# First layer of a two-layer adapter kernel in steps of two groups of batches instead of one

## What is computed

```python
W = weights[condition]                       # 64 x 64 per batch, 16 of them to choose from
c = einsum('bct,bcd->bdt', x, W)             # mixes the 64 tokens of a batch
logits = c @ router_w.T + router_b           # 8 experts
probs = softmax(logits); topv, topi = top_k(probs, 2)
gates = topv / sum(topv)
w = zeros(N, 8) with w[n, topi[n]] = gates[n]
h = einsum('nd,erd->ner', c, A)              # 8 experts x rank 16
out = einsum('ner,eor->no', h * w[:, :, None], Bm) * 0.5
x = x + out
```

## Time and profile before

| | us |
|---|---|
| median of 3 runs (1154.43 to 1160.8) | 1154.85 |
| the profiled execution's own time | 1155.02 |
| its span, first to last instruction | 1153.4 |
| PE busy | 1095.3 (95%) |
| DVE busy | 684.0 (59%) |
| ACT busy | 502.4 (44%) |
| POOL busy | 221.9 (19%) |
| mean granted TensorE clock | 0.989 of full speed |
| last add of the first layer (store issued) | 157.9 from the start |

### The profile page before, as it was taken

One profiled execution on the slowest core, in us unless ns is written; L12 is line 12 of the kernel. 1 busy time (PEld: TensorE's weight loads), 2 busy tenths in 40 slices (PEclk: granted clock), 3 DMA queues, 4 the chain that ended last, 5 costly groups with the idle time before them and its releaser, 6 DMA issues.

```text
span 1153.4 us, 21547 instructions
## 1 busy us (share of the span) xinstructions
PE 1095.3 (95%) x5801; PEld 916.0 (79%) x5802; DVE 684.0 (59%) x1321; ACT 502.4 (44%) x1027; POOL 221.9 (19%) x354
## 2 busy tenths in 40 slices
PE   4899979999999899999999999999999999999998
PEld 4899967888878688778888778777777788888886
DVE  4788953472745628463555486835555466656666
ACT  1112213563745637463565472135555444444443
POOL 2111110020201102010111000055554232222210
PEclk9899989999999999999999999999999999999999
DMA  6489855393665828475664442269999899999995
GB/s 214 165 299 336 274 213 184 113 355 122 237 246 178 286 79 303 157 260 211 220 227 152 152 121 74 73 206 352 356 350 346 334 394 354 334 365 328 314 332 201
DMA packets 114924, 283.09 MB, mean 245 GB/s; under 512 B 17202, under 2 KB 22322, under 8 KB 112946
## 3 DMA queue, kind: packets, MB, share of 16 engines
q1 hardware_dynamic: 85232, 178.95, 44.1%
q0 software_dynamic: 29216, 102.91, 25.6%
q10 hardware_dynamic: 418, 0.53, 0.2%
HBM read 181.65 MB, written 100.70 MB: 245 GB/s over the span
## 4 chain that ended last, share of the span: by engine, by line
PE 65%; DVE 12%; DMA 9%; issue 5%; ACT 3%; SPq 3%; DVEq 1%; ACTq 1%; POOL 0%; POOLq 0%
PE psum L1451 15%; PE psum L1453 15%; PE psum L1452 15%; PE psum L1545 4%; PE psum L1650 3%; PE psum L1651 3%; DMA xp<-act_scratch 3%; DMA out<-x1t 2%; PE psum L1537 2%; DVE x1g L1057 2%; PE psum L1546 2%; PE psum L1461 1%; ACT w L833 1%; PE psum L1659 1%; SPq L503 1%
## 5 line engine op out<-in xcount | busy, mean ns | idle before, releaser
L1451 PE MATMUL psum<-base_hi,xp_hi 128*128 128x512 f32 x512 | 204.7, 400 | 4.8 <-DVE xp_lo L1189 2.7
L1453 PE MATMUL psum<-base_hi,xp_lo 128*128 128x512 f32 x512 | 200.2, 391 | 0.0
L1452 PE MATMUL psum<-base_lo,xp_hi 128*128 128x512 f32 x512 | 200.2, 391 | 0.0
L1451 PE MATMUL psum<-w,xp_hi 128*128 128x512 f32 x448 | 183.5, 410 | 3.1 <-DVE xp_lo L1107 2.4
L1453 PE MATMUL psum<-w,xp_lo 128*128 128x512 f32 x448 | 178.2, 398 | 0.0
L1452 PE MATMUL psum<-w,xp_hi 128*128 128x512 f32 x448 | 177.9, 397 | 0.0
L647 POOL DMA_DIRECT2D raw<-w1T x112 | 59.1, 528 | 437.7 <-DVE w L1089 414.1
L1089 DVE TENSOR_TENSOR w<-raw,w 128x1024 fp32r<-128x1024 f32 x112 | 132.4, 1221 | 14.3 <-ACT w L768 8.0
L815 ACT ACTIVATE xp_hi<-xp 128x256 fp32r<-128x256 f32 x124 | 51.4, 417 | 180.4 <-PE psum L1453 171.3
L1189 DVE TENSOR_TENSOR xp_lo<-xp,xp_hi 128x256 fp32r<-128x256 f32 x124 | 52.0, 425 | 119.9 <-ACT xp_hi L815 119.7
L1451 PEld LDWEIGHTS psum<-base_hi,xp_hi 128*128 128x128 f32 x512 | 96.3, 188 | 30.3 <-issue 5.8
(11 more groups left out here) (278 smaller groups left out, 1952.3 us busy)
## 6 DMA issues: line engine op xcount, KB each, us to landing
raw<-w1T POOLq DMA_DIRECT2D x120, 512.0 KB, 6.5
delta_scratch<-dl SPq DMA_DIRECT2D x80, 512.0 KB, 4.3
xp<-act_scratch SPq DMA_DIRECT2D x74, 256.0 KB, 3.2
act_scratch<-yT SPq DMA_DIRECT2D x72, 256.0 KB, 2.5
act_scratch<-x1g SPq DMA_DIRECT2D x16, 1024.0 KB, 5.2
x1t<-act_scratch SPq DMA_DIRECT2D x64, 256.0 KB, 4.8
out<-x1t SPq DMA_DIRECT2D x62, 256.0 KB, 5.0
xg<-xT SPq DMA_DIRECT2D x15, 1024.0 KB, 8.1
```

The lines of the kernel that those rows point to most:

```text
L1451: mm(out, a_hi, b_hi, start=start, stop=False, skip_group_check=True)
L1452: mm(out, a_hi, b_lo, start=False, stop=False, skip_group_check=True)
L1453: return mm(out, a_lo, b_hi, start=False, stop=stop, skip_group_check=True)
```

## The change

The first layer goes in NS = 8 steps of two groups. The gates of two groups are one chain of small operations on 128 x 32 elements (18 with the two bias additions) and four `hw0`. The mixing result has two banks (1 and 7), the transposed hidden values two halves of bank 2. In step n PE turns groups 2n and 2n+1, projects 2n+3, mixes 2n+2, expands 2n with the mixing of 2n+3 behind its first quarter, expands 2n+1 and projects 2n+4. The loops over steps are written out.

Beside it: the ring of x has six buffers (XRING); `index_3` and the reading of its sums (`index_read`) stand ahead of the first gates; `w0tab` is loaded by SyncE behind x of group 0, and no longer by ScalarE after the first half of it has landed; ScalarE makes the exponent of the next gates ahead of its later projection copy; POOL's early load for the second layer waits for the adds of groups 0 to 11, as its buffer is shared with the ring.

```diff
-RING = 4
+XRING = 6
+NS = NG // 2
+GS = 2 * GT
...
-            act.wait_ge(xg_first[0], 16)
-            for h in range(2):
-                act.dma_start(w0tab[h * C:(h + 1) * C, :], w0).then_inc(w0_in, 16)
...
+            for n in range(NS):
+                h0_high(n)
...
+                if n < NS - 1:
+                    z_copy(2 * n + 3)
+                    if NS - 5 <= n:
+                        w_high(2 * (n - NS + 5), 16)
+                        w_high(2 * (n - NS + 5) + 1, 16)
+                    gates_exp(n + 1)
+                if n < NS - 2:
+                    z_copy(2 * n + 4)
...
-            def step0(g, slot):
-                gates0(g + 1)
-                add_x(g, slot, 0)
-                hidden_low(g + 1)
-                add_x(g, slot, 1)
...
+            for n in range(NS - 1):
+                hidden_low(2 * n)
+                hidden_low(2 * n + 1)
+                if n == 0:
                     index_4()
+                else:
+                    add_x(2 * n - 1, 1)
+                if n == NS - 2:
+                    gates0(n + 1)
+                add_x(2 * n, 0)
+                add_x(2 * n, 1)
+                if n == 1:
+                    dve.wait_ge(const_split_hi, 2)
+                    second_layer_constants()
+                if n < NS - 2:
+                    gates0(n + 1)
+                    add_x(2 * n + 1, 0)
+                if NS - 5 <= n < NS - 2:
+                    w_low(0, 2 * (n - NS + 5))
+                    w_low(0, 2 * (n - NS + 5) + 1)
...
+            def two_groups(n):
+                if n < NS - 1:
+                    turn_h0(n)
+                    z_of(2 * n + 3, 0)
+                    y_of(2 * n + 2)
+                    z_of(2 * n + 3, 1)
+                    if n == 0:
+                        pe.wait_ge(const_split, 1)
+                expand(2 * n)
+                if n == NS - 2:
+                    turn_h0(n + 1)
+                expand(2 * n + 1)
+                if n < NS - 2:
+                    z_of(2 * n + 4, 0)
+                    z_of(2 * n + 4, 1)
```

More of the change, by code:

```diff
@@ L409, in _ @@
                 sp.dma_start(xg[0][:, ks, :], xT[0, :, ks, :]).then_inc(xg_first[q], 16)
+            for h in range(2):
+                sp.dma_start(w0tab[h * C:(h + 1) * C, :], w0).then_inc(w0_in, 16)
             load_x(1, 1)
             sp.dma_start(b0raw[:, :], b0T).then_inc(b0_in, 16)
-            for g in range(2, RING):
+            for g in range(2, 4):
                 load_x(g, g)
@@ L615, in w0_blocks @@
                     w0_block(2 * t + s, s)
-            for g in range(RING):
+            for g in range(4):
                 if g >= 2:
@@ L700, in _ @@
             act.activation(b0_hi[:, :], b0raw[:, :], ACT.Copy).then_inc(const_split_hi, 1)
[L701 to L709, removed]
+            z_copy(1)
+            gates_exp(0)
+            z_copy(2)
+            for n in range(NS):
+                h0_high(n)
+                if n == 0:
+                    act.wait_ge(const_in, 16 * 2)
+                    act.activation(q2[:, :, 0:Z1], q1raw[:, :, :], ACT.Copy).then_inc(const_split_hi, 1)
+                if n < NS - 1:
[6 more added lines that the diff above has]
+                    z_copy(2 * n + 4)
             def x_high(j, half):
@@ L1071, in _ @@
             index_2()
+            index_3()
+            index_read()
             dve.wait_ge(rbias_in, 16)
@@ L1483, in y_of, with expand @@
                 last.then_inc(yz_done, 1)
-            def group0(g, slot, last_group=False):
-                if not last_group:
-                    z_of(g + 1, (slot + 1) % RING, 0)
-                pe.wait_ge(hw0_ready, 2 * g + 2)
-                if not (isinstance(g, int) and g == 0):
-                    pe.wait_ge(h0_lo_done, g)
-                for m in range(GT):
-                    last = pe.transpose(h0T_ps[:, m * P:(m + 1) * P], hw0[:, m, :], ident[:, :])
-                last.then_inc(h0T_done, 1)
-                if not last_group:
-                    z_of(g + 1, (slot + 1) % RING, 1)
-                if isinstance(g, int) and g == 0:
-                    pe.wait_ge(const_split, 1)
+            def expand(g):
@@ new lines, in turn_h0 @@
+            def turn_h0(n):
+                pe.wait_ge(hw0_ready, GS * (n + 1))
+                if n > 0:
+                    pe.wait_ge(h0_lo_done, 2 * n)
+                for m in range(GS):
+                    last = pe.transpose(h0T_of(2 * n + m // GT)[:, m % GT * P:(m % GT + 1) * P], hw0[:, m, :],
+                                        ident[:, :])
+                last.then_inc(h0T_done, 1)
+            def two_groups(n):
[4 more added lines that the diff above has]
+                    z_of(2 * n + 3, 1)
+                    if n == 0:
+                        pe.wait_ge(const_split, 1)
[6 more added lines that the diff above has]
+                    z_of(2 * n + 4, 1)
```

223 lines of the change are left out of this document (120 added, 103 removed).

## The result

The changed kernel takes 1143.8 us in the median of 4 runs (1142.0 to 1146.36), the kernel before 1157.82 beside it (4 runs, 1154.43 to 1161.34): a ratio of 0.988, 95% interval 0.9835 to 0.9925. It is faster by a little over 1%, 13 to 14 us where 15.6 were forecast, and 1143.8 lies within the range. One launch of the kernel before, beside e1 to e4, took 1810.3 us at a mean granted clock of 0.557 and enters no ratio. The profiled execution took 1142.0 us with a span of 1140.4; the one before 1155.02 and 1153.4, so like against like gives 13.0 us.

A forecast was written before the change was run, and what follows sets the result against it. VectorE was taken to set the pace in late groups, and a loop of PE and VectorE early. A last add 16.8 us earlier, less 1.2 of allowances, gained 15.6: 1155.0 to 1139.4 us, range 1136.5 to 1145.5.

The forecast's parts named there:

- Bound: Middle of the first layer: the two-group step becomes PE's own work, with gates hidden by 1.0 us to spare.
- PE's step: PE's work on two groups: transposes 0.5, half projections 7.08, mixings 0.84, expansions 6.06; 14.48 us in all.
- Gates: VectorE's paired chain: small operations at 0.223 us make 3.98, four `hw0` 0.80; 4.8 us for two groups.
- Start: Before the first step: the 4.14 us wait for the mixing matrices goes, first transposes at 29.6.
- Constants: Step 1: the second layer's constants, 2.23 us, stand ahead of the gates; PE waits 1.3 us.
- End: From step 6: PE waits 2.9 us, then VectorE sets the pace; last add at 141.1, 16.8 us earlier.
- Allowances: Clock after the new 2.9 us wait, 0 to 2 us, and DMAs, 0 to 3.6; 1.2 taken for both.
- The sum: Whole launch: a gain of 15.6 us from 1155.0 gives 1139.4 us.
- B: Rival: DMAs bound the early steps, 15.7 us a step, 3.6 us over three steps; 1141.8 us; chance 0.13.
- rival E: Rival: x of odd groups lands late, PE waits in five steps from 11 us landing; 1173 us at 14.7; chance 0.04.
- C: Rival: gates longer than thought, setting the step from 5.8 us on; 6.5 us less gain, 1145.9 us; chance 0.07.
- D: Rival: the start gives less, PE's idle time there could be 4 us more; 1143.5 us; chance 0.06.

The follow-up runs named there:

- e1: Changed kernel with a result-neutral reduction repeated four times in every chain of gates, some 0.9 us more each; 1151.03 us in one run.
- e4: Changed kernel with ScalarE's exponent of the next gates behind its later projection copy; 1157.04 us in one run.
- e2: Changed kernel with fourteen repeats of a reduction in every chain of gates, some 3.1 us more each; 1171.62 us, 1.0112 times the kernel before.
- e5: Changed kernel with `w0tab` loaded by ScalarE's queue again, behind the wait for x's first half; 1148.01 us in one run.
- f1: Kernel before with only the load of `w0tab` moved to SyncE's queue behind x's first tile; 1153.66 us, 0.996 times the kernel before.
- e7: Changed kernel with the second layer's vector constants behind the adds of their step instead of ahead; 1146.75 us in a single run.
- f3: Changed kernel with the second layer's vector constants behind their step's adds, timed in six runs; 1143.37 us, 0.9866 times the kernel before.
- e3: Changed kernel with four buffers of x instead of six; 1275.62 us in one run.
- f2: Changed kernel again without an edit; 1145.85 us in six runs, 0.9888 times the kernel before.
- e8: Changed kernel with VectorE's last two `w_low` behind the last adds; no launch time given, last add 0.1 us earlier against the first transposes.
- e6: Changed kernel with a step's second mixing ahead of the even group's first expansion quarter; 1152.86 us.

## Why the prediction was right, and where its sizes were off

T, S and L are those of the prediction: the end of a step's second mixing, the start of its transposes, and the last add.

*Bound.* Right: PE's step sets the pace of the middle and the gates are hidden in it. e1 shows that 0.9 us more gates cost the middle nothing, e2 that 3.1 cost 2.0. No DMA bounds it.

*PE's step* was the mis-sized term: 14.48 forecast, 14.95 measured. The transposes of four came to 0.74, outside the bounds of 0.28 to 0.56; the four half projections to 7.41, not 7.08, since the half behind the transposes takes 1.93 and the full one 3.71; mixings 0.88 for 0.84; the expansions 5.92, less than 6.06. The rows of single groups, added up, don't give the step; 0.33 us of the difference shows only in steps that begin without a wait. What sets it isn't shown.

*Gates.* Right: 4.04 + 0.80 = 4.84 for the 4.8 forecast, a small operation 0.22 to 0.23 us for 0.223, near the lower bound of 0.207. The value was a choice between two bounds far apart (0.207 and 0.32), so that it came to the third digit is luck. They start at T + 3.05 (2.95) and PE returns at T + 8.83 (8.80).

*Start.* 29.69 for 29.6, but by luck in part: other executions of the same code have 29.97 to 31.39. The order of the steps was right (mixing 0 at 19.22, index sums from 20.10, gates from 24.59). What the table's new place is worth was wrong: in the paired start e5 shows 0.3 us for it, and f1 shows that its 4.5 could be had without any pairing.

*Constants.* 1.3 forecast, 1.22 measured, and e7 shows that they are the cause.

*End.* Step 6's T came at 126.20, not 123.5, by the steps' length and T being 6.12 behind S, not 5.68. From there the last add took 18.0, not 17.6: 0.26 of the difference is a wait for a store. The PE wait was 2.82 for 2.9. So L = 144.2 for 141.1, and the forecast's own sign, a last store at 141 to 143, was missed.

*Allowances.* 1.2 us for the clock and the DMAs. In the first profile the clock stayed up and 0 was due, and that was luck. From the last transposes to the end of the last add it took 12.79 us there; in the other executions with the same order and the same wait, at a clock of 0.50 to 0.83 in the stages behind it, it took 13.17 (e5), 13.39 (f3), 13.40 (e3, e4, e7) and 14.26 (f2). So the clock costs 0.4 to 1.5 us here, within the 0 to 2 of the forecast. The rule of the Trainium skill, page "TensorE: Matmul & The Clock Gate", part "The HAM clock gate", pointed the right way in these six and wasn't borne out by the first profile.

*The sum.* By profiles, 3.1 later at L, less 1.2 not used, and 0.7 lost in the second layer: 2.6 us, the difference between 1139.4 and 1142.0. The medians differ by more (1143.8), since the level it started from was low: the median of the kernel before, 1154.85 in three runs, is 1157.82 in four and 1158.69 in seventeen. The gain, which doesn't depend on the level, was 14.0 and 12.8 by the medians, for 15.6.

*Rivals.* B: the DMA share was 1.01 from 80 to 88 us, yet PE waits for no tile of x. Landing grew, and the loads, issued ahead into a ring of six, covered it. The issues from 84 to 108 us, answering to the earlier trace rows:

```profile
act_scratch<-x1g SPq DMA_DIRECT2D x3, 1024.0 KB, 7.2
xg<-xT SPq DMA_DIRECT2D x3, 1024.0 KB, 9.2
raw<-w1T POOLq DMA_DIRECT2D x2, 512.0 KB, 6.5
```

A load lands in 9.2 us, 8.1 before, and rival E needed 11 to begin. C would have needed gates longer by 1 us. C's price, 1145.9, lies above the range's end of 1145.5, which was said to take it in. The lower end doesn't come out of its own terms either: without the allowance and with a chain shorter by 0.25 us in the three places where it shows, the sum is about 1137.4, not 1136.5. D's price of 4 us at the start didn't come; a variation of 1.7 us did, from the first projection. E became real only in e3, when the ring was four. The earlier place of `index_3` and POOL's later load weren't tried by themselves.

*A rule on the DMAs.* The stage from 12 to 24 us of the changed kernel, in which nearly only loads run:

```profile
12.00:24.00 12.00, 11.25 (x93) 10.31 (x93) 6.66 (x36) 1.85 (x3) 2.79 (x12) 1.00 1.01 403
```

So this core alone moves 403 GB/s from DRAM for 12 us, and 361 with loads and stores mixed from 44 to 52. The Trainium skill, page "DMA: Bandwidth & Descriptors", section "Where 436 GB/s comes from", lets the DRAM side bind near 358 GB/s, while its section "Measured" has 425 for a core alone. By the rows the first is no ceiling for one core; the 403 is nearer to the second.

## What to carry to other kernels

Where an engine's long chain of small dependent operations sits in a loop with another engine, make the chain once for two units of work: eighteen operations on twice the elements cost 4.04 us where two chains cost 7.04, and the pairing pays as long as the chain ends before the other engine returns. Check what the pairing doubles elsewhere (buffers: the ring of four cost 130 us) and where a short operation stands behind a copy that waits for the end of the step (13.5 us). Take the cheap part by itself first: 0.4% of the time, a third of this gain, was to be had by the place of one transfer.

## What the runs showed of the hardware

*The first projection runs at half rate for a time that differs between executions.* Its 32 matmul records took 5.41 us in the first profile, 6.97 in e7. Two stages of 1 us of f2:

```profile
12.00:13.00 1.00, 1.00 (x6) 1.00 (x6) 0.83 (x6) 0.00 (x0) 0.00 (x0) 1.00 0.98 369
...
15.00:16.00 1.00, 1.00 (x11) 1.00 (x10) 0.83 (x4) 0.00 (x0) 0.34 (x2) 1.00 1.05 426
```

Six records in a stage, then eleven (one that lies across an edge counts on both sides), with the clock column at 1.00 in both. Single records of f2 start 0.227 us apart up to 14.7 us and 0.116 apart from 14.9 on, half. The column is no witness ahead of that: the trace's list of granted levels, from which it is made, begins with a full level only at 14.76 us in f2, at 14.26 in the first profile and at 17.60 in e7, and in each of them the records' distance halves within 0.1 us of it. So this is the clock at its lower level. The Trainium skill, page "TensorE: Matmul & The Clock Gate", part "The HAM clock gate", says that the engine starts in the slow state and that the number of slow matmuls differs by run; the traces agree, with 5.41 to 6.97 us for the same 32 records. The end of this projection moves by 1.7 us (16.7 to 18.4), and the first transposes with it.

*The same wait doesn't always lower the clock.* Eight executions have the wait of 2.82 us before the last transposes. In the first profile the clock stayed at 1.00; in the seven others it fell (mean of the stage behind: 0.50 in f2, 0.60 in e8, 0.66 in f3, 0.67 in e3, 0.71 in e5 and e7, 0.74 in e4). After six waits of 2.48 (e4) it stayed up, after one of 2.12 (e1) it fell to 0.73.

*One execution can't tell 1 or 2 us.* From the last add's end to the end of the span it took 995.5 (before), 996.2, 996.1 (e4), 996.3 (e8), 998.5 (e1), 999.2 (f1), 999.4 (f3), 999.6 (e5), 999.7 (e7), 1000.8 (e6), 1000.9 (e3), 1001.7 (f2) and 1002.2 (e2), with the same second layer. The two profiles of the changed kernel differ by 7.3 us in span; span times (1 - mean clock) is 8.0 for the one (0.993) and 14.9 for the other (0.987), so the granted clock could account for nearly all of it. What makes the clock differ stays open.
